# Third and fourth normalisation, step sizes and gate logits by batches in the experts' loop and the mixer's steps; batches stored singly

## The chip, the cores and the metric

The kernel runs on one core of a Trainium2 chip. The metric is the device time of one execution in microseconds (us). A core has five engines with a queue of instructions each: TensorE (PE: matrix products and transposes through the array into PSUM), VectorE (DVE), ScalarE (ACT), GpSimd (POOL) and SyncE (SP, which here issues the transfers by DMA). Each works through its own queue in order and waits for others by semaphores. SBUF is the working memory; PSUM holds eight banks of results.

## The reference, cut to what matters

```python
x = L0_attn_a_x                       # 8 x 512 x 128, float32
x = x + attention(layernorm(x))
x = x + experts(layernorm(x))
x = x + mixer(layernorm(x))
x = x + experts(layernorm(x))         # the same weights again

def layernorm(x):  return (x - mean(x)) / sqrt(var(x) + 1e-5)

def experts(x):                       # 4096 tokens, 8 experts
    probs = softmax(x @ wg)
    idx = argmax(probs)
    # a token is kept if it is among the first 512 of its expert
    gate = probs[idx] * kept
    return gate * (x @ W[idx].T + b[idx])

def mixer(u):                         # a state-space mixer, 8 heads
    z, xBC, dt = split(u @ W_in.T)
    dt = softplus(dt + dt_bias)
    x, B, C = split(silu(conv(xBC) + conv_b))
    y = scan(x * dt, A * dt, B, C) + x * Dskip
    return (layernorm(concat(y, z)) * ln_w + ln_b) @ W_out
```

## The kernel before

The stream x stays in SBUF for the whole program (`k.X`, named `stream` in the trace), 32 tiles of 128 tokens each, 128 wide. Four tiles are a group, which is also one of the 8 sequences. `k.XNT` (`stream_normed_t`) holds the normalised stream, turned, so that its tiles can go into TensorE. The stages come one after the other: attention, experts, mixer, experts. Within a stage each engine has its own program, written out by hand in the order in which the engine does it; there is no scheduler.

**Normalising.** The first two normalisations are done by groups inside other work, with the `group_` functions (L185 to L255): `group_stats` (DVE: four statistics L207, four merges L211, the variance L214), `group_rstd` (POOL, L220), `group_scale` (DVE, four operations L227), `group_turn` (PE, four transposes L238), `group_keep` (ACT, L245) and `group_products` (PE, L252: the matrix of 8 columns that the next stage needs, in bank 7). The third and fourth are done by `norm` (L1934) as stages of their own: `norm_vector`, `norm_gpsimd`, `norm_tensor` and `norm_scalar` (L99 to L177) take the stream in two halves. Behind them `eight_tensor` (L1222) multiplies all 32 tiles by a matrix of 8 columns: the mixer's raw step sizes behind the third, the gate logits of the second experts stage behind the fourth.

**Experts** (L1236). From the logits (L1315) a chain on DVE makes the gates (`gate8`, `experts_gate`; the last operation is L1340). Then a loop over the 8 groups, two at a time. SP copies the group's normalised tiles and its gates into small buffers (L1349, L1352). TensorE turns the gates (L1363), then for each tile makes two products of 512 columns, one for experts 0 to 3, "near", and one for 4 to 7, "far" (L1373), in two pairs of banks; behind the first tile come the products of gates and biases (L1382). DVE multiplies the near half by its gates out of PSUM (L1426), ScalarE the far half (L1401), and DVE adds the two (L1418); it also adds the biases to the stream (L1435). When the four tiles are there, POOL sums the eight experts' parts in two steps (L1448, L1451) and adds them to the stream (L1456).

A near bank is free for TensorE's next but one tile when DVE has multiplied (`near_scaled`), a far bank when ScalarE has (`far_scaled`).

**Mixer** (L1468). A chain on DVE makes the step sizes from the raw ones. Then steps, one for each sequence and shifted against each other: step i brings in sequence i+1 (projections, convolution), runs the scan over the tiles of sequence i, and finishes sequence i-1 (normalised y, output product, addition into the stream, L1877). At the end of a step DVE has in its queue the last addition L1877, the products behind the activations (L1817 to L1822) and the four operations of the normalised y (L1921).

**End.** `store_stream` (L1959) writes the whole stream by one transfer of 2048 KB.

## Time and profile before

| | us |
|---|---|
| median of 3 runs | 2992.06 (2991.2 to 2996.38) |
| profiled execution | 2988.63, of which its span 2986.9 |
| first experts stage: gates, loop | 2359.9 to 2369.5, to 2451 |
| third normalisation, step sizes' products | 2451 to 2473.4, to 2487.6 |
| mixer's steps | 2496.2 to 2850.6 |
| fourth normalisation, logits' products | 2850.9 to 2873, to 2887.3 |
| second experts stage: gates, loop | 2887.3 to 2896.9, to 2977.5 |
| store | 2977.8 to 2986.9 |

All before 2351 us is the attention and the first two normalisations. Over the whole span DVE is busy 90%, TensorE 85%, POOL 75% and ScalarE 69% of the time. These shares are those of the attention; the last fifth of the span is another program, and its stretches have to be read one by one. In the rows below a line such as "x4" puts several like instructions together: the time before the engine's name is then the sum of all of them. What stands in brackets at the end is how long the engine sat idle before, and what it waited for.

### The profile page before, as it was taken

The page shows a single profiled execution, that of the slowest core. Times are in us where ns is not written, and L with a number is a line of the kernel's source. Part 1 is how long each engine was busy: PE and PEld are TensorE (multiplying, and loading weights), DVE is VectorE, ACT ScalarE, POOL GpSimd, SP SyncE. Part 2 cuts the span into 40 slices and gives each one's busy share as a digit, 9 for nine tenths or more (in the row PEclk, how much of TensorE's full clock was granted, in tenths as well). Part 3 has the DMA queues.
Part 4 walks back from the last instruction along what each step waited for, and adds up shares of the span by engine and source line. Part 5 has one row for each costly group of instructions (what it writes and reads, how often), then busy time and mean ns, then how long its engine had stood idle before and what let it go on. Part 6 is the DMA issues. An engine that isn't in the chain of part 4 may idle for free. (4 is left out here: it accounts for less than half of the span.)

```text
span 2986.9 us, 56920 instructions
## 1 busy us (share of the span) xinstructions
PE 2534.7 (85%) x16480; PEld 1489.4 (50%) x16480; DVE 2680.1 (90%) x6614; ACT 2062.6 (69%) x6275; POOL 2254.1 (75%) x2816
## 2 busy tenths in 40 slices
PE   5788888888888888888888888888888777988857
PEld 3444444444444444444544444444444436777743
DVE  7999999999999999999999999999999374776546
ACT  3788888888888788888887878888887342222214
POOL 4899999998998999999999989999998251222105
PEclk8899999999999999999999999999999786776659
DMA  4444444444444444444444444444443000000001
GB/s 123 121 120 118 121 121 120 121 121 120 120 121 115 120 119 124 121 123 119 122 117 118 123 117 120 122 120 124 119 121 101 12 19 15 8 8 0 1 12 47
DMA packets 373454, 286.18 MB, mean 96 GB/s; under 512 B 30174, under 2 KB 369192, under 8 KB 373160
## 3 DMA queue, kind: packets, MB, share of 16 engines
q1 hardware_dynamic: 372232, 280.62, 33.0%
q8 instruction: 129, 2.11, 0.3%
q10 hardware_dynamic: 928, 2.10, 0.2%
q14 instruction: 165, 1.35, 0.1%
HBM read 139.48 MB, written 136.58 MB: 92 GB/s over the span
## 5 line engine op out<-in xcount | busy, mean ns | idle before, releaser
L1038 DVE MAX8 top<-work 128x8 f32<-128x512 f32 x1536 | 982.8, 684 | 0.0
L1047 DVE MATCH_REPLACE8 work<-top,work 128x512 f32<-128x512 f32 x1024 | 687.4, 682 | 0.0
L1124 POOL TENSOR_TENSOR scores<-scores,cut 128x512 f32<-128x512 f32 x512 | 642.0, 1276 | 0.0
L657 PE MATMUL bank<-probs_t,u 128*64 128x512 f32 x2048 | 476.8, 608 | 10.9 <-ACT u L893 1.4
L1116 POOL TENSOR_SCALAR cut<-scores,minus_max_and_least 128x512 f32<-128x512 f32 x512 | 354.2, 692 | 46.9
L945 ACT ACTIVATE probs_of_tile<-scores,minus_max_and_least 128x512 f32<-128x512 f32 x512 | 376.2, 767 | 14.4 <-POOL scores L1124 14.4
L1137 POOL TENSOR_SCALAR probs_of_tile<-probs_of_tile,inverse 128x512 f32<-128x512 f32 x512 | 349.2, 692 | 26.9 <-DVE inverse L1004 1.4
L1047 DVE MATCH_REPLACE8 work<-top,scores 128x512 f32<-128x512 f32 x512 | 343.6, 682 | 0.0
L1035 DVE MAX8 top<-scores 128x8 f32<-128x512 f32 x512 | 326.7, 683 | 5.2 <-ACT scores L886 4.9
L1120 POOL TENSOR_SCALAR cut<-cut 128x512 f32<-128x512 f32 x512 | 305.6, 613 | 21.5
L864 ACT ACTIVATE band<-band 128x129 f32<-128x129 f32 x512 | 155.2, 304 | 225.1 <-DMA band<-probs_scratch 224.2
L886 ACT ACTIVATE scores<-bank 128x512 f32<-128x512 f32 x512 | 273.3, 584 | 45.1 <-PE bank L706 45.0
L910 ACT ACTIVATE probs_t<-bank 128x512 f32<-128x512 f32 x512 | 282.0, 609 | 11.4 <-PE bank L753 10.3
L753 PE MATMUL bank<-identity,probs_of_tile 128*128 128x128 f32 x2048 | 278.4, 281 | 4.1 <-POOL probs_of_tile L1137 4.1
L657 PEld LDWEIGHTS bank<-probs_t,u 128*64 128x64 f32 x2048 | 137.8, 139 | 267.8 <-issue 228.0
L741 PE MATMUL bank<-identity,band 128*128 128x128 f32 x512 | 109.8, 297 | 185.5 <-ACT band L873 184.1
L657 PE MATMUL bank<-probs_t,v 128*64 128x384 f32 (+1 forms) x2048 | 255.4, 392 | 0.0
L753 PEld LDWEIGHTS bank<-identity,probs_of_tile 128*128 128x128 f32 x2048 | 242.7, 145 | 4.5 <-POOL probs_of_tile L1137 4.5
L657 PEld LDWEIGHTS bank<-probs_t,v 128*64 128x64 f32 x2048 | 124.3, 139 | 173.1 <-ACT probs_t L910 99.0
L1769 POOL TENSOR_TENSOR mixer_a_spread<-rest_after,mixer_a 128x1024 f32<-128x1024 f32 x32 | 66.4, 2075 | 168.8 <-PE bank L1626 137.6
L678 PE MATMUL bank<-keys_left,qt 64*128 64x64 f32 (+3 forms) x1024 | 185.5, 439 | 1.3 <-ACT scores L886 1.3
L923 ACT ACTIVATE rel<-bank 128x254 f32<-128x254 f32 x512 | 174.3, 414 | 1.9 <-PE bank L694 1.9
(274 smaller groups left out, 5005.6 us busy)
## 6 DMA issues: line engine op xcount, KB each, us to landing
probs_scratch<-probs_of_tile SPq DMA_DIRECT2D x256, 256.0 KB, 2.4
band<-probs_scratch SPq DMA_DIRECT2D x256, 256.0 KB, 3.2
rel_scratch<-rel SPq DMA_DIRECT2D x256, 254.0 KB, 3.1
relj<-rel_scratch SPq DMA_DIRECT2D x256, 128.0 KB, 2.3
relj<-rel_scratch SPq DMA_DIRECT2D x512, 64.0 KB, 2.4
experts_xs<-stream_normed_t SPq DMA_DIRECT2D x16, 256.0 KB, 2.3
stream<-in_L_attn_a_x SPq DMA_DIRECT2D x4, 512.0 KB, 7.9
mixer_xs<-stream_normed_t SPq DMA_DIRECT2D x8, 256.0 KB, 2.4
```

The costliest lines, as they stand in the source:

```text
L657: last = nc.tensor.matmul(U[HEADS[h], lo:hi], lhs, pt[mpar][:, h, jt, lo:hi], start=(jt == 0 and lo == 0), stop=(jt == NT - 1 and step > 0))
L753: last = nc.tensor.transpose(PT[h][:, jt * P:(jt + 1) * P], t.prob[Td][:, h, HALF + jt * P:HALF + (jt + 1) * P], k.ident[:, :])
L886: nc.scalar.activation(sc[Tb][:, h, :], SC[h][:, :], ACT.Copy).then_inc(s.scores_kept, 1)
L910: nc.scalar.activation(pt[dpar][:, h, :, Td * P:(Td + 1) * P], PT[h][:, :].rearrange("p (j i) -> p j i", j=NT), ACT.Copy).then_inc(s.probs ...
L945: nc.scalar.activation(t.prob[Tx][:, h, HALF:HALF + N], sc[Tx][:, h, :], ACT.Exp, bias=neg[q][:, h, 0:1], accum_out=rs[Tx][:, h:h + 1]).th ...
L1035: nc.vector.max(top[q][:, h, 0:8], sc[Tc][:, h, :]).then_inc(s.tops, 1)
L1038: nc.vector.max(top[q][:, h, 8 * rnd:8 * rnd + 8], work[:, h, :]).then_inc(s.next_tops, 1)
L1047: nc.vector.match_replace(out=work[:, h, :], in_to_replace=top[q][:, h, 8 * rnd:8 * rnd + 8], in_values=sc[Tc][:, h, :] if rnd == 0 else w ...
L1116: nc.gpsimd.tensor_scalar(cut[:, h, :], sc[Tc][:, h, :], neg[q][:, h, 1:2], STEEP, ALU.add, ALU.mult).then_inc(s.compared, 1)
L1120: nc.gpsimd.tensor_scalar(cut[:, h, :], cut[:, h, :], 0.0, NEG, ALU.min, ALU.max).then_inc(s.cut, 1)
L1124: nc.gpsimd.tensor_tensor(sc[Tc][:, h, :], sc[Tc][:, h, :], cut[:, h, :], ALU.add).then_inc(s.masked, 1)
L1137: nc.gpsimd.tensor_scalar(row, row, inv[Ty][:, h:h + 1], 1.0, ALU.mult, ALU.mult).then_inc(s.probs, 1)
```

## The change

`norm`, its functions, `eight_tensor`, `eight_vector` and `store_stream` are gone. The third normalisation is done by groups inside the first experts loop, the fourth inside the mixer's steps, with the `group_` functions; the raw step sizes and the gate logits come out of `group_products` or of its like in the mixer. All these loops are written out. In detail:

- *Experts' loop.* TensorE and ScalarE read `k.XNT` and `gate8` themselves; the small buffers and SP's copies are gone. The near half's product and the addition become one: four operations `scalar_tensor_tensor` of 128 columns, near out of PSUM times its gate plus the far half (L1299 of the changed kernel). The near bank is free after these (`summed`). The turned gates and the biases have one bank each instead of two, since one bank is needed for turning the group (TURN) and one for the 8-column products (EIGHT).
- *First experts loop only.* In group i DVE does the statistics of group i-1 behind the third tile and its scaling behind the fourth; POOL its `group_rstd` behind its addition; TensorE turns group i-2 between the gates' turns and the first tile and multiplies it behind the third tile; ScalarE keeps it behind the first tile. The last two groups are turned and multiplied behind the loop.
- *Mixer.* In step i DVE does the statistics of sequence i-1 behind the last addition into its stream and its scaling behind the normalised y. TensorE turns sequence i-2 before the projections, in their bank, and multiplies it at the step's end; ScalarE keeps the logits for the second experts stage. There is one step more.
- *Second experts loop.* SP stores each group, 256 KB, when its addition is done.

```diff
-            two_at_a_time(pe, GROUPS, body, with_half=True)
+            for i in range(GROUPS):
+                par = i % 2
+                if i:
+                    pe.wait_ge(g_kept, i)
                 for c in range(4):
-                    last = nc.tensor.transpose(ps[4 + par][0:E, c * P:(c + 1) * P], gs[par][:, c * E:(c + 1) * E],
-                                               k.ident[:, :])
+                    at = (i * 4 + c) * E
+                    last = nc.tensor.transpose(GT[0:E, c * P:(c + 1) * P], b.gate8[:, at:at + E], k.ident[:, :])
                 last.then_inc(g_turned, 1)
+                if follow and i >= 2:
+                    late(i - 2)
                 for c in range(4):
+                    t = i * 4 + c
                     for q in range(2):
-                            pe.wait_ge((near_scaled, far_scaled)[q], i * 4 + c - 1)
+                        if t >= 2:
+                            pe.wait_ge((summed, far_scaled)[q], t - 1)
...
+                    if c == 2 and follow and i >= 2:
+                        group_products(nc, pe, follow, i - 2, follow.W, k.XNT, EIGHT)
+            if follow:
+                for i in range(GROUPS - 2, GROUPS):
+                    late(i)
+                    group_products(nc, pe, follow, i, follow.W, k.XNT, EIGHT)
...
+            def scale(i):
+                if i >= 2:
+                    dve.wait_ge(follow.turned, i - 1)
+                group_scale(nc, dve, follow, gw, k.X, i, gw.xn[:, i % 2, :])
...
-                    nc.vector.tensor_tensor(near[c % 2][:, :].rearrange("p (e f) -> p e f", e=4),
-                                            ps[2 * (c % 2)][:, :].rearrange("p (e f) -> p e f", e=4),
-                                            b.gate8[:, bass.ds(t * E, 4)].unsqueeze(2).to_broadcast([P, 4, P]),
-                                            ALU.mult).then_inc(near_scaled, 1)
+                    for e in range(4):
+                        cols = slice(e * P, (e + 1) * P)
+                        last = nc.vector.scalar_tensor_tensor(
+                            out=sums[par][:, c, cols], in0=ps[2 * (c % 2)][:, cols],
+                            scalar=b.gate8[:, t * E + e:t * E + e + 1], in1=far[c % 2][:, cols],
+                            op0=ALU.mult, op1=ALU.add)
+                    last.then_inc(summed, 1)
...
+                    if c == 2 and follow and i:
+                        stats(i - 1)
+                if follow and i:
+                    scale(i - 1)
```

and in the mixer:

```diff
@@ TensorE
                     first_half(cur, par, 1)
+                if (done := i - 2) >= 0:
+                    if cur is not None:
+                        pe.wait_ge(m.conv_in, cur * 3 + 1)
+                    group_turn(nc, pe, follow, done, gw.xn[:, done % 2, :], PX, k.ident, 1)
                 if front is not None:
                     projections(front, 1 - par, pairs)
...
+                if done >= 0:
+                    pe.wait_ge(follow.kept, done + 1)
+                    if cur is not None:
+                        pe.wait_ge(m.turned_used, (cur + 1) * NT)
+                    for c in range(NT):
+                        t = done * NT + c
+                        last = nc.tensor.matmul(T1[:, 3 * P + c * E:3 * P + (c + 1) * E], k.XNT[:, t * P:(t + 1) * P],
+                                                follow.W, start=True, stop=True)
+                    last.then_inc(follow.products, 1)
@@ DVE
                     into_stream(NT - 1)
+                    dve.wait_ge(m.out_added, (back + 1) * NT)
+                    group_stats(nc, dve, follow, gw, k.X, back)
                 if front is not None:
                     silu(front, 1 - par)
...
+                if back is not None:
+                    if back >= 2:
+                        dve.wait_ge(follow.turned, back - 1)
+                    group_scale(nc, dve, follow, gw, k.X, back, gw.xn[:, back % 2, :])
```

What the change moves stands below at three places. In these lists a name behind `waits` is a semaphore, its first part the stage or normalisation that it belongs to. First TensorE at the start of a group of the first experts loop, before (the group's number is 1):

```order
L1363 MATMUL bank<-identity,experts_gs 8x128 [waits experts1_gs_in1]
L1363 MATMUL bank<-identity,experts_gs 8x128 x3
L1373 MATMUL bank<-rest_we,experts_xs 128x512 [waits experts1_near_scaled,experts1_xs_in1]
L1373 MATMUL bank<-rest_we,experts_xs 128x512 [waits experts1_far_scaled]
L1382 MATMUL bank<-rest_eb,experts_gt 128x128 [waits experts1_g_kept]
L1382 MATMUL bank<-rest_eb,experts_gt 128x128 x3
```

and on the same engine at the start of group 2 now:

```order
L1226 MATMUL bank<-identity,experts_gate 8x128 [waits experts1_g_kept]
L1226 MATMUL bank<-identity,experts_gate 8x128 x3
L132 MATMUL bank<-identity,group_xn 128x128 [waits norm3_scaled]
L132 MATMUL bank<-identity,group_xn 128x128 x3
L1235 MATMUL bank<-rest_we,stream_normed_t 128x512 [waits experts1_summed]
L1235 MATMUL bank<-rest_we,stream_normed_t 128x512 [waits experts1_far_scaled]
L1243 MATMUL bank<-rest_eb,experts_gt 128x128 [waits experts1_bias_added,experts1_g_kept]
L1243 MATMUL bank<-rest_eb,experts_gt 128x128 x3
```

The turn of the group before last (L132) now stands ahead of the first tile and waits for `norm3_scaled`; the first tile waits for `experts1_summed` instead of `experts1_near_scaled`.

Second, DVE at the end of group 1 of the same loop, before, where `bank0` and `bank2` are the near halves of the third and the fourth tile:

```order
L1426 TENSOR_TENSOR experts1_near0<-bank0,experts1_gate8 128x512 [waits experts1_summed,experts1_near_made]
L1418 TENSOR_TENSOR experts1_sums1<-experts1_near1,experts1_far1 128x512 [waits experts1_far_scaled,experts1_near_scaled]
L1426 TENSOR_TENSOR experts1_near1<-bank2,experts1_gate8 128x512 [waits experts1_summed,experts1_near_made]
L1418 TENSOR_TENSOR experts1_sums1<-experts1_near0,experts1_far0 128x512 [waits experts1_far_scaled,experts1_near_scaled]
L1418 TENSOR_TENSOR experts1_sums1<-experts1_near1,experts1_far1 128x512 [waits experts1_far_scaled,experts1_near_scaled]
```

and on DVE there now:

```order
L1299 SCALAR_TENSOR_TENSOR experts1_sums1<-bank0,experts1_gate8,experts1_far0 128x128 [waits experts1_far_scaled,experts1_near_made]
L1299 SCALAR_TENSOR_TENSOR experts1_sums1<-bank0,experts1_gate8,experts1_far0 128x128 x3
L101 BN_STATS group_stats<-stream 128x6 [waits experts1_stream_added]
L101 BN_STATS group_stats<-stream 128x6 x3
L105 BN_AGGR group_mean_var<-group_stats 128x2 [waits norm3_stats]
L105 BN_AGGR group_mean_var<-group_stats 128x2 x3
L108 TENSOR_SCALAR group_vareps<-group_mean_var 128x4 [waits norm3_merged]
L1299 SCALAR_TENSOR_TENSOR experts1_sums1<-bank2,experts1_gate8,experts1_far1 128x128 [waits experts1_far_scaled,experts1_near_made]
L1299 SCALAR_TENSOR_TENSOR experts1_sums1<-bank2,experts1_gate8,experts1_far1 128x128 x3
L121 TENSOR_SCALAR group_xn<-stream,group_mean_var,group_rstd 128x128 [waits norm3_rstd]
L121 TENSOR_SCALAR group_xn<-stream,group_mean_var,group_rstd 128x128 x3
```

The statistics of the group before stand between the third and the fourth tile, its scaling (L121) behind the fourth; every tile's first product waits for ScalarE's `far_scaled`.

Third, DVE at the end of a step of the mixer, before:

```order
L1877 TENSOR_TENSOR stream<-bank,stream 128x128 [waits mixer_out_made]
L1817 SCALAR_TENSOR_TENSOR mixer_x<-mixer_tanh_x,mixer_half_x 128x512 [waits mixer_squashed]
L1820 SCALAR_TENSOR_TENSOR mixer_b<-mixer_tanh_bc,mixer_half_bc 16x512 [waits mixer_squashed]
L1822 SCALAR_TENSOR_TENSOR mixer_c<-mixer_tanh_bc,mixer_half_bc 16x512
L1921 TENSOR_SCALAR mixer_yn<-mixer_yz,mixer_n_mean,mixer_n_rstd 128x256 [waits mixer_yn_turned,mixer_rstd]
L1921 TENSOR_SCALAR mixer_yn<-mixer_yz,mixer_n_mean,mixer_n_rstd 128x256 x3
```

and on DVE there now:

```order
L1773 TENSOR_TENSOR stream<-bank,stream 128x128 [waits mixer_out_made]
L101 BN_STATS group_stats<-stream 128x6 [waits mixer_out_added]
L101 BN_STATS group_stats<-stream 128x6 x3
L105 BN_AGGR group_mean_var<-group_stats 128x2 [waits norm4_stats]
L105 BN_AGGR group_mean_var<-group_stats 128x2 x3
L108 TENSOR_SCALAR group_vareps<-group_mean_var 128x4 [waits norm4_merged]
L1713 SCALAR_TENSOR_TENSOR mixer_x<-mixer_tanh_x,mixer_half_x 128x512 [waits mixer_squashed]
L1716 SCALAR_TENSOR_TENSOR mixer_b<-mixer_tanh_bc,mixer_half_bc 16x512 [waits mixer_squashed]
L1718 SCALAR_TENSOR_TENSOR mixer_c<-mixer_tanh_bc,mixer_half_bc 16x512
L1819 TENSOR_SCALAR mixer_yn<-mixer_yz,mixer_n_mean,mixer_n_rstd 128x256 [waits mixer_yn_turned,mixer_rstd]
L1819 TENSOR_SCALAR mixer_yn<-mixer_yz,mixer_n_mean,mixer_n_rstd 128x256 x3
L121 TENSOR_SCALAR group_xn<-stream,group_mean_var,group_rstd 128x128 [waits norm4_rstd,norm4_turned]
```

Nine operations of statistics stand ahead of the activations' products and four of scaling behind the normalised y.

## Rows read from the trace of the kernel before

**Rows 1.** Timeline at the third normalisation: start us, us, engine line operation.

```profile
2449.70 1.26 POOL L1456 TENSOR_TENSOR stream<-experts_one_sum,stream 128x512 f32 x1 [0.26 <-POOL experts_one_sum L1451]
...
2487.57 0.42 DVE L1233 COPY mixer_raw<-bank 128x256 f32<-128x256 f32 x1 [16.04 <-PE bank L1227]
```

**Rows 2.** Timeline at the fourth normalisation.

```profile
2850.25 0.29 DVE L1877 TENSOR_TENSOR stream<-bank,stream 128x128 f32<-128x128 f32 x1 [2.96 <-PE bank L1676]
...
2887.72 0.42 DVE L1317 TENSOR_REDUCE experts_top<-experts_logit 128x32 f32<-128x256 f32 x1
```

**Rows 3.** Timeline at the second normalisation's end, where the last group passes.

```profile
2349.28 0.60 PE L238 MATMUL bank<-identity,keys_left 128*128 128x128 f32 x4
...
2351.01 0.96 PE L252 MATMUL bank<-rest_wg,stream_normed_t 128*128 128x8 f32 x8
...
2351.46 0.87 DVE L207 BATCH_NORM_STATS2 group_stats<-stream 128x6 f32<-128x128 f32 x4 [20.36 <-POOL stream L1097]
...
2354.09 1.12 DVE L227 TENSOR_SCALAR keys_right<-stream,group_mean_var,group_rstd 128x128 f32<-128x128 f32 x4 [1.13 <-POOL group_rstd L220]
...
2355.26 1.11 PE L238 MATMUL bank<-identity,keys_right 128*128 128x128 f32 x4 [3.29 <-DVE keys_right L227]
...
2359.91 0.42 DVE L1315 COPY experts_logit<-bank 128x256 f32<-128x256 f32 x1 [4.70 <-PEq L582]
```

**Rows 4.** Timeline of one group in the first experts loop.

```profile
2418.11 1.88 PE L1373 MATMUL bank<-rest_we,experts_xs 128*128 128x512 f32 x4
...
2420.00 2.35 POOL L1448 TENSOR_TENSOR experts_two_sums<-experts_sums 128x1024 f32<-128x1024 f32 x1 [3.22 <-DVE experts_sums L1418]
...
2421.00 5.42 PE L1373 MATMUL bank<-rest_we,experts_xs 128*128 128x512 f32 x12
...
2423.23 1.14 ACT L1401 ACTIVATE experts_far<-bank,experts_gate 128x128 f32<-128x128 f32 x4 [1.88 <-PE bank L1373]
...
2428.58 2.35 POOL L1448 TENSOR_TENSOR experts_two_sums<-experts_sums 128x1024 f32<-128x1024 f32 x1 [3.22 <-DVE experts_sums L1418]
```

**Rows 5.** Busy time by stretch: the mixer's steps, one step's end.

```profile
core 0: us, PE busy (x) PEld busy (x) DVE busy (x) ACT busy (x) POOL busy (x), PEclk, DMA share, GB/s
2496.20:2850.60 354.40, 305.20 (x1568) 249.45 (x1568) 226.35 (x635) 94.40 (x184) 74.78 (x40) 0.69 0.02 7
2666.00:2676.00 10.00, 9.05 (x55) 6.58 (x54) 9.94 (x22) 3.96 (x7) 3.94 (x2) 0.94 0.00 0
```

**Rows 6.** Timeline at the first experts loop's start.

```profile
2369.10 0.42 DVE L1340 TENSOR_TENSOR experts_gate<-experts_keep,experts_prob 128x256 f32<-128x256 f32 x1
...
2370.03 0.55 SPq L1349 DMA_DIRECT2D experts_xs<-stream_normed_t  x1
...
2372.59 1.02 PE L1363 MATMUL bank<-identity,experts_gs 128*8 128x128 f32 x4 [7.51 <-DMA experts_gs<-experts_gate]
...
2373.40 3.62 PE L1373 MATMUL bank<-rest_we,experts_xs 128*128 128x512 f32 x4
```

**Rows 7.** Timeline in the mixer: DVE out of PSUM at 128 columns.

```profile
2633.84 0.28 DVE L1843 TENSOR_TENSOR mixer_dtx<-bank,mixer_dt 128x128 f32<-128x128 f32 x1
...
2634.04 0.28 DVE L1844 TENSOR_TENSOR mixer_yz<-bank,rest_dskip 128x128 f32<-128x128 f32 x1
```

**Rows 8.** Two lines at 38 us: durations in ns, least, median, most.

```profile
L227 DVE TENSOR_SCALAR probs_t<-stream,group_mean_var,group_rstd x4: 1291/1301/1307, 38.1 to 41.8; 128x128 f32<-128x128 f32 x4
L1068 POOL TENSOR_TENSOR stream<-stream,attention_out_bias x8: 1256/1262/1268, 38.1 to 46.6; 128x512 f32<-128x512 f32 x8
```

**Rows 9.** Timeline at one step's end in the mixer.

```profile
2667.08 3.02 DVE L1921 TENSOR_SCALAR mixer_yn<-mixer_yz,mixer_n_mean,mixer_n_rstd 128x256 f32<-128x256 f32 x4
...
2667.41 1.90 POOL L1769 TENSOR_TENSOR mixer_a_spread<-rest_after,mixer_a 128x1024 f32<-128x1024 f32 x1 [1.51 <-PE bank L1626]
```

**Rows 10.** Transfers: KB each, median us from issue to landing.

```profile
probs_scratch<-probs_of_tile SPq DMA_DIRECT2D x256, 256.0 KB, 2.4
out_stream<-stream SPq DMA_DIRECT2D x1, 2048.0 KB, 8.7
```

More of the change, by code:

```diff
@@ L1408, in _, with stats @@
+            if follow:
+                for i in range(GROUPS - 2, GROUPS):
+                    group_keep(nc, act, follow, i, TURN, k.XNT)
         @block.vector
         def _(dve):
-            def body(i, par, first):
-                def add(c):
-                    t = i * 4 + c
-                    dve.wait_ge(near_scaled, t + 1)
-                    dve.wait_ge(far_scaled, t + 1)
-                    if c == 0 and not first:
-                        dve.wait_ge(stream_added, i - 1)
-                    nc.vector.tensor_tensor(sums[par][:, c, :], near[c % 2][:, :], far[c % 2][:, :],
-                                            ALU.add).then_inc(summed, 1)
+            def stats(i):
+                dve.wait_ge(stream_added, i + 1)
+                group_stats(nc, dve, follow, gw, k.X, i)
@@ L1759, in body @@
                         keep_turned(back, c)
+                if done >= 0:
+                    act.wait_ge(follow.products, done + 1)
+                    nc.scalar.activation(follow.logits[:, done * NT * E:(done + 1) * NT * E],
+                                         T1[:, 3 * P:3 * P + NT * E], ACT.Copy).then_inc(m.logits_kept, 1)
             run_steps(act, body)
```

273 lines of the change are left out of this document (77 added, 196 removed).

## Prediction

> **What bounds the kernel now.** I read four views, in this order: busy time by stretch, the timeline at each seam, the timeline of one steady group of the experts' loop, and the costs of a few single forms. The attention, up to 2351 us, is not touched. The last 635 us are.
>
> At each of the two late normalisations the program stands. The third: the last addition into the stream ends at 2449.70 + 1.26 = 2450.96, and the raw step sizes are copied at 2487.57 [rows 1]. In these 36.6 us the whole stream is normalised, turned and multiplied. The fourth: 2850.25 + 0.29 = 2850.54 to the reduction of the logits at 2887.72, 37.2 us [rows 2]. What such a seam costs when the earlier groups have been done beforehand, the second normalisation shows, which already works so: from its last group's statistics at 2351.46 to the copy at 2359.91, 8.45 us [rows 3].
>
> In the experts' loop TensorE sets the pace. One group lies between POOL's two first sums at 2420.00 and 2428.58, 8.58 us; TensorE works in it from 2418.11 to 2426.42, 8.31 us, and the other engines have room [rows 4]. In the mixer no engine rules alone: TensorE is busy 305.20 of 354.40 us at a granted clock of 0.69, DVE 226.35, but in the ten microseconds at the end of a step DVE is busy 9.94 of 10.00 [rows 5].
>
> **The change part by part**, against the profiled execution (2988.63 us, which is 3.4 under the median of the runs).
>
> *Third normalisation's seam.* 36.6 us go, 8.45 come for the last group: **-28.2**. *Fourth:* 37.2 go; 8.45 come, with 0.2 for the hop to ScalarE, which now keeps the logits in the loop: **-28.5**.
>
> *The loads in front of the two loops.* The gates are done at 2369.10 + 0.42 = 2369.52, and TensorE starts at 2372.59, after the gates' transfer [rows 6]: 3.1 us. Now TensorE reads the gates directly. About 0.6 us stay for the start of the block; this estimate is the 0.5 us between the gates' end and the first transfer's issue at 2370.03 [rows 6], and a hop. **-2.5 twice, -5.**
>
> *The near half's bank, both loops.* It was freed by DVE's product alone. Now it is freed by four products of 128 columns which also add the far half, so they wait for ScalarE: 1.14 us for its four activations [rows 4]. Such a product of 128 columns with PSUM, a gate and an SBUF operand does not occur in the trace. Nearest are two forms from PSUM at 128 columns, 0.28 us each and 0.20 apart [rows 7]; the bounds are 4 x 0.20 and 4 x 0.34, and I take 1.1. With some 0.45 for three hops the bank is free 2.7 us after the far half is made; until then TensorE has one tile to do, 5.42 / 3 = 1.81 [rows 4]. Per group one tile pays the 0.9 in full (the third tile is covered by the bias products, the next group's first by the gates' turns). 8 x 0.9 = **+7** for the second loop, where this is all that happens; by the two bounds of the products it is +5 and +9.
>
> *The first loop's new wait.* This is the largest term. In group i TensorE, after turning the gates, has to turn the normalised group i-2 before its first tile. That group was scaled by DVE as its last work in group i-1, behind the products of the last tile. So TensorE can't run into group i while DVE finishes group i-1, as it does now; the engines go one after the other. The chain of one group is then:
> - TensorE from the first tile to the last: 8.31 as before [rows 4], and four products of the following stage, 0.96 [rows 3]: 9.3.
> - ScalarE 1.14, four products 1.1, hops 0.45: 2.7.
> - DVE's scaling, four operations on SBUF. Alone they take 1.12 [rows 3]. But here POOL starts its three sums at the same moment, because both are released by the same last product. Where the same scaling ran beside POOL's 1.26-us additions, at 38 us, each of the four took 1.30 instead of 0.28 [rows 8]: they went one and one. Here the first meets the sum of 2.35 us [rows 4], the other three the shorter ones: 2.35 + 3 x 1.29 = 6.2. Bounds 1.1 and 6.2. I take 6.2, as the row nearest in kind has no overlap left.
> - The turn, 0.60 at full clock [rows 3].
> - The clock. TensorE now sits idle 8.9 us (2.7 + 6.2) in each group. After an idle time of 7.51 us the first tile took 3.62 instead of 1.88 [rows 4, 6], and even after 3.29 us a turn took 1.11 instead of 0.60 [rows 3]: near the lower level (1.2 instead of 2.4 GHz). That is 1.7 + 0.5, **+2.2**.
>
> Sum 9.3 + 2.7 + 6.2 + 0.6 + 2.2 = 21.0 us a group, against 8.6: +12.4 for each of the groups 2 to 7, 74 us. The first two groups pay the bank's wait (+2) and the last group, whose chain begins after a late DVE, some +2 more (estimates): **+78**. The statistics (1.5 us: from 2351.46 to 2354.09 less the 1.13 that DVE then waits for POOL [rows 3]) stand behind the third tile and are covered: DVE waits there for TensorE. That two transfers a group fall away gives nothing more, since TensorE waited only for the first.
>
> *The mixer.* DVE gets, between the last addition of a step and the activations' products, statistics of 1.5 us, and behind the normalised y a scaling of 1.12 [rows 3]; both lie in the stretch where DVE is busy without a gap [rows 5], and the first matrices of the next step wait for the products behind it. 2.6 x 7 = 18. The four operations of the y, next to which it stands, take 3.02 beside POOL's spreading of 1.90 [rows 9], so the scaling may cost 3 instead of 1.1: upper bound 18 + 13. TensorE gets a turn and four products, 1.6 us a step; in the likeliest case they hide in the waits for DVE at a step's start, and at worst cost 11. Writing the loop out saves its branches, which show no time of their own. **+19.**
>
> *Storing singly.* One transfer of 2048 KB takes 8.7 us; one of 256 KB takes 2.4 [rows 10]. Seven of eight are issued a group apart, 9.5 us, and only the last is waited for: **-6**. The Trainium skill, "DMA: Bandwidth & Descriptors", section "Bandwidth", speaks against this: it tells one to batch transfers to 1 MiB or more. If the eight queued behind one another, at 2.4 each, they would end some 11 us later than the one. That would need a loop faster than its own transfers, and 9.5 is above 2.4.
>
> **Sum:** -28.2 - 28.5 - 5 + 7 + 78 + 19 - 6 = +36.3; 2988.6 + 36.3 = 3024.9, and with the 3.4 to the median 3028.
>
> **The rivals.** *Scaling and sums don't alternate.* If the four scalings come through in 1.1, a group costs 21.0 - 5.1 = 15.9, 7.3 more than now: 6 x 7.3 + 4 = 48 instead of 78, time 2998. For it: DVE has its scaling next in its own queue, while POOL needs a hop, so DVE may be through before POOL's first sum. Against it: the scaling at 38 us, where all four operations were stretched [rows 8].
> *The other side, faster.* Without the alternation TensorE's idle time is only 3.8 us a group. If the clock is held through that, the group costs 9.3 + 2.7 + 1.1 + 0.6 = 13.7, 5.1 more than now: 31 + 4 = 35. The sum is then -7 with the mixer at +19, and -21 if the mixer's added work fell into DVE's waits but for 5 us: 2971 to 2985. It decides where the group stays below 15 us: seams, loads and store give 67.7, the second loop and the mixer take 26, and of the 41.7 left 4 go to the loop's ends and 6.3 to each of six groups. Against it: the clock was down after 3.29 us of idling [rows 3].
> *The clock stays down through the whole first loop.* Then TensorE's 9.3 double, of which 1.7 are counted: (9.3 - 1.7) x 6 = 46, 3074. Against it: before, it came back one tile after the start.
> *The change doesn't do what it says:* if the waits for a former group left nothing early, the seams would stay at 37 and the added work come on top, over 3050. The order of the instructions speaks against it.
>
> **How the numbers follow.** Forecast as summed: 0.55, its own range 3005 to 3047 (the mixer from +5 to +36, the bank from +5 to +9, the scaling from 5 to 6.2). No alternation 0.17, split by its own width into slower 0.05, same 0.10, faster 0.02. Faster 0.18. Clock down 0.08. No effect 0.02. The predicted time is the forecast's, 3028. The range reaches down to 2978, into the middle of the faster case, and up to 3050: about 0.1 is left out on either side. A measurement of this kernel can tell some 0.2% from no change, 2986 to 2998. Faster 0.20, the same 0.10, slower 0.70.
>
> **What would show it.** In the changed kernel's first loop TensorE should wait, in front of the turn, for the scaled group, 8 to 9 us in each of six groups, and its first tile after that should be at half clock. The scaling should show four operations of over a microsecond while POOL sums. The second loop should have a period near 9.5. Both seams should be near 8.5. The steps of the mixer should grow by 2.6. The prediction is wrong if the scaling takes 1.1 and TensorE waits under 4 us, or if the turn finds its group already scaled.

## The result, and the profile after

The changed kernel takes 3027.43 us (median of 4 runs, 3012.61 to 3031.43) against 2991.63 us (median of 4, 2988.97 to 2996.38); the ratio is 1.0123, with a 95% interval from 1.0091 to 1.0156. It is slower, as forecast, and the time lies in the range. The ratio is taken over all runs of both kernels and can differ a little from the quotient of the medians, here and below. Its profiled execution has a span of 3022.6 us, 35.7 more than before. The stretches, each from one profile, ends taken from the last row of the stage:

| stretch | before | after | difference | forecast |
|---|---|---|---|---|
| attention up to the first gates' end | 2369.5 | 2359.3 | -10.2 | 0 |
| first experts loop (gates' end to last addition) | 81.4 | 163.4 | +82.0 | +75.5 |
| third normalisation's seam | 36.6 | 7.9 | -28.7 | -28.2 |
| step sizes and mixer | 363.0 | 385.8 | +22.9 | +19 |
| fourth normalisation's seam | 37.2 | 8.1 | -29.1 | -28.5 |
| second gates | 9.2 | 9.2 | 0 | 0 |
| second experts loop | 80.6 | 86.3 | +5.7 | +4.5 |
| store | 9.4 | 2.7 | -6.7 | -6 |

(The loops' forecasts contain the -2.5 of the loads.) The two seams answer [rows 1, 2]. The third, timeline:

```profile
2521.39 1.26 POOL L1332 TENSOR_TENSOR stream<-experts_one_sum,stream 128x512 f32<-128x512 f32 x1
...
2522.68 0.87 DVE L101 BATCH_NORM_STATS2 group_stats<-stream 128x6 f32<-128x128 f32 x4
...
2525.37 1.11 DVE L121 TENSOR_SCALAR group_xn<-stream,group_mean_var,group_rstd 128x128 f32<-128x128 f32 x4 [1.21 <-POOL group_rstd L114]
2526.55 1.11 PE L132 MATMUL bank<-identity,group_xn 128*128 128x128 f32 x4
...
2530.54 0.42 DVE L1382 COPY mixer_raw<-bank 128x256 f32<-128x256 f32 x1 [4.05 <-PEq L1205]
```

Only the last group's chain fills the seam, in the order of [rows 3]; the turn and the products of the group before it lie beside it. 2521.39 + 1.26 to 2530.54 is 7.9 us.

Where the time went, one group of the first loop shows, also timeline; it answers [rows 4]:

```profile
2426.15 0.60 PE L1226 MATMUL bank<-identity,experts_gate 128*8 128x128 f32 x4
...
2428.63 5.30 DVE L121 TENSOR_SCALAR group_xn<-stream,group_mean_var,group_rstd 128x128 f32<-128x128 f32 x4
2428.80 2.37 POOL L1324 TENSOR_TENSOR experts_two_sums<-experts_sums 128x1024 f32<-128x1024 f32 x1 [0.31 <-DVE experts_sums L1299]
2431.25 1.26 POOL L1327 TENSOR_TENSOR experts_one_sum<-experts_two_sums 128x512 f32<-128x512 f32 x1
2432.59 1.26 POOL L1332 TENSOR_TENSOR stream<-experts_one_sum,stream 128x512 f32<-128x512 f32 x1
2433.99 1.12 PE L132 MATMUL bank<-identity,group_xn 128*128 128x128 f32 x4 [7.24 <-DVE group_xn L121]
2434.90 3.62 PE L1235 MATMUL bank<-rest_we,stream_normed_t 128*128 128x512 f32 x4
...
2438.45 1.15 PE L1243 MATMUL bank<-rest_eb,experts_gt 8*128 8x128 f32 x8
...
2439.53 3.70 PE L1235 MATMUL bank<-rest_we,stream_normed_t 128*128 128x512 f32 x8
...
2448.44 2.37 POOL L1324 TENSOR_TENSOR experts_two_sums<-experts_sums 128x1024 f32<-128x1024 f32 x1 [0.31 <-DVE experts_sums L1299]
```

TensorE has turned the gates at 2426.75 and stands until the scaling is done, 7.24 us. The four scaling operations last 5.30 us, to 2433.93; POOL's third sum ends at 2433.85. Then the turn takes 1.12 and the first tile 3.62, near half speed, and the group comes to 2448.44 - 2428.80 = 19.6 us. The next one takes 23.3. Busy time by stretch for these two (columns as in [rows 5]):

```profile
2428.80:2448.44 19.64, 12.41 (x40) 6.40 (x40) 11.64 (x31) 5.49 (x18) 5.91 (x4) 0.83 0.00 0
2448.44:2471.70 23.26, 16.02 (x40) 8.22 (x40) 11.65 (x31) 5.49 (x18) 5.92 (x5) 0.63 0.00 0
```

TensorE, DVE and ScalarE do the same work in both (POOL's fifth instruction in the second is cut by the stretch's edge); the granted clock is 0.83 and 0.63. The waits of TensorE over the whole loop and the seam behind it, by cause (us in total, times, longest):

```profile
PE bank L132 <- DVE group_xn L121: 51.6, 7, 7.7
PE bank L1235 <- DVE experts_sums L1299: 1.5, 2, 0.7
```

### The profile page after: what moved, and what is told of

Read it like the earlier page. It is cut to its first block and busy times, and to the rows that moved or that the text cites. A ratio compares the mean times of both kernels' runs of the same rounds, so it can differ in the third digit from the quotient of the medians.

```text
span 3022.6 us, 55798 instructions
## 1 busy us (share of the span) xinstructions
PE 2553.1 (84%) x16480; PEld 1492.0 (49%) x16480; DVE 2686.3 (89%) x6791; ACT 2062.5 (68%) x6283; POOL 2259.2 (75%) x2828
## 5 line engine op out<-in xcount | busy, mean ns | idle before, releaser
L932 DVE MAX8 top<-work 128x8 f32<-128x512 f32 x1536 | 1065.6, 792 | 0.0
L941 DVE MATCH_REPLACE8 work<-top,work 128x512 f32<-128x512 f32 x1024 | 742.5, 790 | 0.0
L839 ACT ACTIVATE probs_of_tile<-scores,minus_max_and_least 128x512 f32<-128x512 f32 x512 | 376.4, 767 | 17.5 <-POOL scores L1018 17.5
L941 DVE MATCH_REPLACE8 work<-top,scores 128x512 f32<-128x512 f32 x512 | 370.9, 788 | 0.0
L929 DVE MAX8 top<-scores 128x8 f32<-128x512 f32 x512 | 353.7, 789 | 0.1
L647 PE MATMUL bank<-identity,probs_of_tile 128*128 128x128 f32 x2048 | 272.1, 277 | 4.0 <-POOL probs_of_tile L1031 4.0
L941 DVE MATCH_VALUE_LOAD work<-top,work 128x8 f32 x1024 | 195.2, 191 | 0.0
```

The costliest lines, as they stand in the source:

```text
L647: last = nc.tensor.transpose(PT[h][:, jt * P:(jt + 1) * P], t.prob[Td][:, h, HALF + jt * P:HALF + (jt + 1) * P], k.ident[:, :])
L839: nc.scalar.activation(t.prob[Tx][:, h, HALF:HALF + N], sc[Tx][:, h, :], ACT.Exp, bias=neg[q][:, h, 0:1], accum_out=rs[Tx][:, h:h + 1]).th ...
L929: nc.vector.max(top[q][:, h, 0:8], sc[Tc][:, h, :]).then_inc(s.tops, 1)
L932: nc.vector.max(top[q][:, h, 8 * rnd:8 * rnd + 8], work[:, h, :]).then_inc(s.next_tops, 1)
L941: nc.vector.match_replace(out=work[:, h, :], in_to_replace=top[q][:, h, 8 * rnd:8 * rnd + 8], in_values=sc[Tc][:, h, :] if rnd == 0 else w ...
```

## The experiments

Theory A is the prediction's: the third normalisation makes the engines hand on to each other in the first loop. TensorE waits in front of its first tile for the scaling, the scaling is stretched by POOL's sums, and TensorE's clock is down afterwards. Rivals: B, the added work itself fills the group; C, the clock alone makes it long. The kernel before was run beside them on each chip and lay at 2973.8 to 2986.3 there (medians of 8 to 16 runs), so kernels from different chips are compared by their ratio to it.

| run | median us | range | before on that chip | ratio (95% interval) |
|---|---|---|---|---|
| e1, sums behind scaling | 2978.6 | 2976.2 to 2987.0 | 2986.3 | 0.9967 (0.9952 to 0.9982) |
| e2, turn behind second tile | 2973.1 | 2972.0 to 2977.0 | 2986.3 | 0.9958 (0.9944 to 0.9973) |
| e3, third apart | 2983.3 | 2975.8 to 2986.8 | 2986.3 | 0.9983 (0.9972 to 0.9995) |
| e4, scaling beside statistics | 2951.9 | 2946.6 to 2957.1 | 2986.3 | 0.9887 (0.9868 to 0.9906) |
| e5, TensorE busy | 2990.8 | 2985.2 to 2991.8 | 2973.8 | 1.0052 (1.0027 to 1.0078) |
| e8, buffers kept | 3023.0 | 3010.0 to 3028.7 | 2973.8 | 1.0152 (1.0113 to 1.0190) |
| e9, changed kernel again | 3018.3 | 3010.3 to 3024.3 | 2973.8 | 1.0149 (1.0116 to 1.0183) |
| e6, more statistics | 2967.7 | 2952.0 to 2976.5 | 2981.6 | 0.9955 (0.9932 to 0.9978) |
| e7, near apart | 2938.2 | 2933.2 to 2940.5 | 2981.6 | 0.9856 (0.9834 to 0.9878) |
| e10, before again | 2979.9 | 2975.6 to 2986.0 | 2979.4 | 1.0001 (0.9983 to 1.0020) |
| e11, fourth apart | 2944.7 | 2932.3 to 2950.4 | 2979.4 | 0.9877 (0.9838 to 0.9915) |
| e12, near apart again | 2942.3 | 2932.4 to 2945.8 | 2979.4 | 0.9880 (0.9851 to 0.9908) |

**e1: the sums behind the scaling.**

```diff
                 if i:
                     pool.wait_ge(stream_added, i)
+                    if follow:
+                        pool.wait_ge(follow.scaled, i)
                 nc.gpsimd.tensor_tensor(two_sums[:, :, :, :], four[:, :, 0:2, :], four[:, :, 2:4, :],
```

> The changed kernel with one wait more: in the first experts loop POOL starts a group's sums only when DVE's scaling of the group before is done. Theory A (TensorE waits in front of its first tile for the scaling, and the scaling is stretched because it alternates with POOL's sums): the four scaling operations fall from 5.3 to 1.1 us, TensorE's wait in front of the turn from 7.2 to some 3.0, each of seven groups is 4.2 us shorter, with up to 1.7 more where a tile gets its full clock back: 29 to 39 us off, 2988 to 2998. Rival B (the new work of DVE and the later release of the banks fill the group by themselves, and the alternation lies beside them): no change within 5 us, 3022 to 3032; or slower by the 1.1 us a group that the sums start later.

One wait more makes the kernel some 47 us faster than the changed one (0.9967 against 1.0123 of before). Theory B falls, since the added work is all still there. A is right in kind, and its forecast of 29 to 39 us was too small. The first of the two groups below, timeline, takes 13.3 us:

```profile
2432.96 0.66 PE L132 MATMUL bank<-identity,group_xn 128*128 128x128 f32 x4 [3.05 <-DVE group_xn L121]
2433.08 2.35 POOL L1326 TENSOR_TENSOR experts_two_sums<-experts_sums 128x1024 f32<-128x1024 f32 x1 [1.43 <-DVE group_xn L121]
2433.45 1.88 PE L1235 MATMUL bank<-rest_we,stream_normed_t 128*128 128x512 f32 x4
...
2445.11 1.10 DVE L121 TENSOR_SCALAR group_xn<-stream,group_mean_var,group_rstd 128x128 f32<-128x128 f32 x4
2446.27 1.11 PE L132 MATMUL bank<-identity,group_xn 128*128 128x128 f32 x4 [3.05 <-DVE group_xn L121]
2446.38 2.34 POOL L1326 TENSOR_TENSOR experts_two_sums<-experts_sums 128x1024 f32<-128x1024 f32 x1 [1.43 <-DVE group_xn L121]
```

The scaling takes 1.10 and the wait 3.05, as expected. What I had not counted is the clock: after the same idle time of 3.05 us the turn took 0.66 in one group and 1.11 in the next. The seven groups took 11.3, 14.9, 15.1, 13.0, 13.3, 17.8 and 13.3.

**e2: the turn behind the second tile.**

```diff
-                if follow and i >= 2:
-                    late(i - 2)
...
+                    if c == 1 and follow and i >= 2:
+                        late(i - 2)
-                    if c == 2 and follow and i >= 2:
+                    if c == 3 and follow and i >= 2:
                         group_products(nc, pe, follow, i - 2, follow.W, k.XNT, EIGHT)
```

> The changed kernel with TensorE's turn of group i-2 moved from in front of group i's first tile to behind its second, the 8-column products from behind the third tile to behind the fourth, ScalarE's copy with them. The scaling stays where it is, stretched by POOL. Theory A: TensorE makes two tiles while DVE scales; what is left of a group is DVE's chain, 5.3 of scaling, 1.1 and 0.7 for the first tile and the biases, 3.3 until the third tile is there, 1.1, 1.4 of statistics, 1.1, some 13 to 14 us instead of 22.4: six groups give 50 to 56, 2971 to 2977. Rival B (the work fills the group): the group stays over 20 us, 3015 or more. Rival C (the clock is what makes the groups long, not the wait): the group falls by no more than 4, 3003 or more.

As theory A has it, and against C: groups of 13.1, 13.4, 15.3, 14.9, 14.6 and 13.4 us, 2973.1. The scaling is as long as ever; it only isn't waited for:

```profile
2429.06 5.39 DVE L121 TENSOR_SCALAR group_xn<-stream,group_mean_var,group_rstd 128x128 f32<-128x128 f32 x4
2429.08 2.34 POOL L1324 TENSOR_TENSOR experts_two_sums<-experts_sums 128x1024 f32<-128x1024 f32 x1
...
2430.57 1.98 PE L1233 MATMUL bank<-rest_we,stream_normed_t 128*128 128x512 f32 x4
...
2434.50 0.66 PE L132 MATMUL bank<-identity,group_xn 128*128 128x128 f32 x4 [1.95 <-DVE group_xn L121]
```

TensorE makes tiles while DVE scales, and 1.95 us of the wait are left.

**e3: the third normalisation put back as a stage of its own.**

```diff
-            norm3.W = r.wdt[:, :]
-            experts(nc, sem, allocate(ctx), ps, k, r, "experts1", norm2, norm3, gw)
+            experts(nc, sem, allocate(ctx), ps, k, r, "experts1", norm2)
+        norm(nc, norms, ps, k, w)
```

> The changed kernel with the third normalisation and the step sizes' products put back as stages of their own, by the code of before; the fourth, the stores and the near halves stay changed. If the first loop's loss is the handing on of the third normalisation and nothing else, this loop takes what the second one does, 86 us instead of 163, and the seam is 36.6 again instead of 7.9: 77 off, 29 on, 2979. If the loss came from the near halves' product or from reading gates and stream directly, the loop stays well over 100 us, and the time at 3000 or more.

All seven groups of the first loop take 9.6, the loop 86.8, the seam 36.4; the time, 2983.3, is 4 above the expected. So of the first loop's 82 us the third normalisation makes 76.6 (163.4 against 86.8); the rest is the near bank's, as in the second loop.

**e4: both ends moved.**

```diff
                     if c == 2 and follow and i:
+                        dve.wait_ge(stream_added, i)
+                        if i >= 2:
+                            scale(i - 2)
                         stats(i - 1)
-                if follow and i:
-                    scale(i - 1)
```

and on TensorE and ScalarE the turn of group i-3 behind the second tile, its products behind the fourth.

> The changed kernel with both ends moved in the first loop: DVE scales group i-2 in group i right before the statistics of i-1, when POOL has no sum to make, and TensorE turns group i-3 behind the second tile of group i. Theory A: scaling 1.1, no wait in front of the first tile, a group of 9.6 to 10.5 like the second loop's: 70 to 75 off and 2 to 4 on for a third group after the loop, 2955 to 2962, faster than the kernel before. Rival B: DVE has 7.7 us of work in a group, which stand between tiles, so that the tiles are released later: 12 or more a group, 2975 or more. Rival C: the clock does not come back, 18 or more a group, 3000 or more.

Groups of 10.1 to 10.4, the loop 94.9, and 2951.9: faster than the kernel before by 1.1% (0.9 to 1.3). The time is 3 us below the expected range, but on this chip the kernel before is some 5 us faster too. The scaling is short and nobody waits for the turn:

```profile
2419.73 0.60 PE L132 MATMUL bank<-identity,group_xn 128*128 128x128 f32 x4
...
2424.38 1.10 DVE L121 TENSOR_SCALAR group_xn<-stream,group_mean_var,group_rstd 128x128 f32<-128x128 f32 x4
```

**e5: TensorE kept busy.** Seven products whose results are overwritten, in front of the turn:

```diff
                 if follow and i >= 2:
+                    if i >= 3:
+                        pe.wait_ge(follow.kept, i - 2)
+                    for n in range(7):
+                        nc.tensor.matmul(TURN[:, :], k.XNT[:, i * 512:i * 512 + P], r.we[:, 0:512], start=True, stop=True)
                     late(i - 2)
```

> The changed kernel with seven products of 512 columns more in front of each of the six turns that wait, written into the turn's bank, which the turn then overwrites: TensorE works through most of the 7.2 us in which it waited, and nothing else is moved. Theory: of the changed kernel's 22.4 us a group some 4 to 5 are the lower clock after the wait (the groups took 19.6 to 23.7, and those with one slow tile less were the shorter). With TensorE working the turn takes 0.6 and the first tiles 1.9, a group 17 to 18: 25 to 32 off the changed kernel, 2995 to 3002. Rival: the clock has nothing to do with it and the length is all waiting: no change within 5 us of the changed kernel in this call, or longer where the added products end after the scaling.

The kernel does more and is faster by 27 us than the changed kernel on the same chip (2990.8 against 3018.3). All six groups take 17.5:

```profile
2404.77 0.66 PE L132 MATMUL bank<-identity,group_xn 128*128 128x128 f32 x4 [1.24 <-DVE group_xn L121]
2405.27 1.88 PE L1239 MATMUL bank<-rest_we,stream_normed_t 128*128 128x512 f32 x4
...
2414.86 6.17 PE L1232 MATMUL bank<-rest_we,stream_normed_t 128*128 128x512 f32 x14
...
2416.91 5.30 DVE L121 TENSOR_SCALAR group_xn<-stream,group_mean_var,group_rstd 128x128 f32<-128x128 f32 x4
```

The added products are those of L1232; the scaling is stretched as before, and the turn waits for it. But the turn takes 0.66 and the first tile 1.88. So of a group's 21 to 22 us some 4 to 5 are the clock, and 17.5 are what the work and the handing on take at full clock, against 9.6 without the third normalisation (e3). C holds for the smaller part.

**e6: more statistics in the mixer**, on e4's kernel.

```diff
                     dve.wait_ge(m.out_added, (back + 1) * NT)
+                    for n in range(8):
+                        t = back * NT + n % NT
+                        nc.vector.bn_stats(spare[:, n, :], k.X[:, t * D:(t + 1) * D])
                     group_stats(nc, dve, follow, gw, k.X, back)
```

> The kernel of the fourth experiment with eight statistics more, into a spare buffer, in front of the eight group statistics of the mixer's steps: 8 x 0.21 us, 1.7 us of DVE more a step at the very place where the change put its 1.5. Theory D (the end of a step is DVE's, as the prediction had it): every step grows by 1.7, 12 to 14 us in all, 2964 to 2966. Rival E (once the steps run at some 44.5 us, TensorE at its lower clock sets their length and DVE's work lies beside it; only the steps before that and the last grow): 2 to 7 us, 2954 to 2959, and the steps of 44.5 stay as they are.

Neither theory holds as a whole. The time is some 20 us above e4's by the ratios (0.9955 against 0.9887), more than D would have it, but runs of this kernel lie 24 us apart. In its profile the fourth to the seventh step stay at 44.4, as E would have it, and the first three grow to 41.4, 44.0 and 47.3 (e4: 39.0, 40.3, 44.1). So the steps of 44.4 have room for 1.7 us more of DVE at this place. What makes the others longer stays open.

**e7: the near half's product and addition apart in the second loop**, on e4's kernel.

```diff
-                            pe.wait_ge((summed, far_scaled)[q], t - 1)
+                            pe.wait_ge((near_scaled if out is not None else summed, far_scaled)[q], t - 1)
```

and DVE's instructions for this loop as they were before.

> The kernel of the fourth experiment with the near halves' product and their addition apart again in the second experts loop, as in the kernel before, so that a near bank is free after DVE's product alone. If the later release of the near bank is what makes a group 9.60 instead of 8.58, the loop falls to 8.6 a group: 7 to 8 off, 2944 to 2945. If the direct reading of gates and stream or the single banks for gates and biases make it, a group stays at 9.6: no change within 2.

All seven groups of the second loop take 8.6 and the loop 77.8 instead of e4's 87.7. Two of POOL's first sums, timeline, in the changed kernel's second loop:

```profile
2957.31 2.35 POOL L1324 TENSOR_TENSOR experts_two_sums<-experts_sums 128x1024 f32<-128x1024 f32 x1 [4.56 <-DVE experts_sums L1299]
...
2966.91 2.35 POOL L1324 TENSOR_TENSOR experts_two_sums<-experts_sums 128x1024 f32<-128x1024 f32 x1 [4.57 <-DVE experts_sums L1299]
```

and in e7's:

```profile
2886.93 2.35 POOL L1354 TENSOR_TENSOR experts_two_sums<-experts_sums 128x1024 f32<-128x1024 f32 x1 [3.21 <-DVE experts_sums L1289]
...
2895.51 2.35 POOL L1354 TENSOR_TENSOR experts_two_sums<-experts_sums 128x1024 f32<-128x1024 f32 x1 [3.21 <-DVE experts_sums L1289]
```

The loop's added microsecond a group is the near bank's later release. At 2938.2 this is the lowest median of all kernels here, 1.4% (1.2 to 1.7) under the kernel before, though its interval overlaps that of e4; run again as e12, 1.2% (0.9 to 1.5):

> The kernel of the seventh experiment, unaltered, beside the two others on one chip: 2933 to 2941 as then, groups of 10.1 to 10.4 us in the first experts loop and 8.6 in the second, steps between 375 and 386, gates done between 2358 and 2363.

In e12's profile the gates were done at 2356.3, below the expected 2358; its median is 1 us above the expected range, and the loops' groups are as expected.

**e8, e9 and e10: the 10 us of the attention.** e8 allocates the former buffers again, without using them; e9 and e10 are the changed kernel and the one before, unaltered.

> The changed kernel with the buffers of the former normalisation still allocated at their old place and not used, so that what is allocated behind them has its old addresses. In the two profiles the first experts stage's gates were done 10.2 us earlier in the changed kernel, at 2359.3 instead of 2369.5, though all before that is the same code. Theory (addresses): gates done at 2367 to 2370 here, the time 8 to 10 above the changed kernel in this call. Rival (one execution differs from another by that much): gates at any time between 2358 and 2370, the time within 5 of the changed kernel.

> The changed kernel itself, unaltered, for comparison on the same chip: by its first measurement 3012 to 3031, its median 3027. By the theory on addresses its gates are done within 2 us of 2359.3; by the rival they may be done up to 10 later.

> The kernel before, unaltered, for a second profile of it. In nine profiles of kernels with the changed mixer its steps take 375 to 386 us, 381 in the mean, against 363.0 in the one profile of before. If the added work makes that difference, the steps take 360 to 367 here again; if one execution differs from another by that much, they may take up to 380. By the theory on addresses the first experts stage's gates are done between 2365 and 2370, as in the three profiles of kernels that hold the old buffers, and not between 2358 and 2363 as in the seven that do not.

The gates were done at 2365.8 in e8 and 2359.7 in e9, which spoke for the addresses. But e10, with the very code of before, had them done at 2361.2, against 2369.5 in its first profile: the same program differs by 8 us there from one execution to another, and the times of e8 and e9 agree within their intervals. So the 10.2 us are not shown to be the addresses'. Nor is an effect of theirs excluded: on each of the three chips that ran both kinds, every kernel that holds the old buffers had its gates done later than every one that doesn't, by 5 to 9 us. That is 2368.0 (e3) against 2358.9 to 2362.9 (e1, e2, e4), 2365.8 (e8) against 2358.4 and 2359.7 (e5, e9), and 2361.2 and 2363.2 (e10, e11) against 2356.3 (e12). With one profile each this stays open.

**e11: the fourth normalisation put back as a stage of its own**, on e7's kernel.

```diff
-            mixer(nc, sem, allocate(ctx), ps, k, r, norm3, norm4, gw)
+            mixer(nc, sem, allocate(ctx), ps, k, r, norm3, None, gw)
+        norm(nc, norms, ps, k, w)
```

> The kernel of the seventh experiment with the fourth normalisation and the gate logits put back as stages of their own, by the code of before, so that the mixer's steps are those of before. Theory (the mixer pays 18 for the fourth normalisation and the seam gives 29): steps 363 instead of 381, the seam 37.2 instead of 8.1: 5 to 17 slower than the seventh experiment's kernel in this call, some 2949. Rival (the steps' length comes from the clock and not from the added work, they take 375 to 386 without it too): the whole seam is lost, 25 to 30 slower, 2965.

2944.7 against e12's 2942.3: no difference that these runs can tell. In the profiles the seam is 36.8 against 8.1, and step sizes and mixer take 353.1 against 376.7. So what the seam gives, 29 us, the mixer takes back all but some 5. The theory's 5 to 17 us in the whole time don't show. The rival falls: without the added work the stretch is short, 363.0, 360.9 (e10) and 353.1, while the ten profiles with the fourth normalisation in it and nothing added (the changed kernel, e1 to e5, e7, e8, e9, e12) lie between 375.2 and 385.8, 380.7 in the mean. The steps of e11 do the work of those of before, but they are written out like the changed kernel's, where the kernel before has a loop for the middle ones. So e11 against e12 shows the added work by itself, 23.6 us. Whether the 8 to 10 us by which e11 lies under the kernel before come from the writing out, one profile doesn't show.

## Why the prediction was right, point by point

**The seams, the loads, the store**: -28.7, -29.1, 0.5 us in place of 3.1 in front of each loop, and -6.7. All as worked out. The loads at the first loop, timeline; it answers [rows 6]:

```profile
2358.86 0.43 DVE L1201 TENSOR_TENSOR experts_gate<-experts_keep,experts_prob 128x256 f32<-128x256 f32 x1
...
2359.83 1.01 PE L1226 MATMUL bank<-identity,experts_gate 128*8 128x128 f32 x4 [5.00 <-PEq L1152]
```

The last 256 KB are through 2.7 us after the last addition, where the one large transfer was through 9.4 after it. Of the eight small ones seven lie beside the loop, and they don't queue up: they land 2.3 us after their issue in the median, and are issued 9.6 apart.

**The near bank.** A group of the second loop takes 9.60 instead of 8.58, 1.0 each where I had 0.9; the four products take 1.13 together (forecast 1.1). e7 shows the cause.

**The first loop's wait.** This is the step that decided the sign, and it went as described: the turn in front of the first tile, waiting for a scaling that is last in DVE's row, stretched by POOL (e1, e2, e3). Of its terms the scaling was 5.30 and not 6.2: it starts 0.17 us ahead of POOL's first sum, so the first of the four passes freely, and the last ends with POOL's last sum. The wait was 7.24 and not 8.9; the forecast had not taken off the gates' turns (0.60), which TensorE does before it. The clock was mis-sized the other way: I had one turn and one tile at the lower level, 2.2 us. In the changed kernel sometimes the biases' products and the second tile were slow too. This is the row of the group that begins at 2406.76, timeline:

```profile
2412.86 3.62 PE L1235 MATMUL bank<-rest_we,stream_normed_t 128*128 128x512 f32 x4
2416.42 2.07 PE L1243 MATMUL bank<-rest_eb,experts_gt 8*128 8x128 f32 x8
...
2418.42 5.17 PE L1235 MATMUL bank<-rest_we,stream_normed_t 128*128 128x512 f32 x8
```

The biases take 2.07 instead of the 1.15 at 2438.45, and the next two tiles 5.17 instead of the 3.70 at 2439.53. By e5 the clock's share is 4 to 5 us a group. The two errors, -0.9 and +2 to 3, partly cancelled, which is luck: 21.0 forecast, 22.4 measured in the mean of groups 2 to 7, and 21.2 in e9's profile. How many products are slow differs from execution to execution: the loop took 163.4, 157.2 and 159.9 us in the changed kernel's two profiles and in e8's. The 19 us by which runs of the changed kernel spread are not explained by that, since the kernel before spreads by 16 to 25 us on the other chips too.

**The mixer.** The total was near, +22.9 in the first profile, and +18.7 between the mean of the ten profiles and that of the two of the kernel before (363.0 and 360.9). The working was not, so the agreement is luck: "2.6 x 7" lets every step grow alike. Busy time by stretch, for the second step, the seventh, and the last to its last addition, columns as in [rows 5]. Before:

```profile
2551.18:2590.93 39.75, 37.37 (x202) 29.93 (x202) 27.22 (x80) 11.78 (x23) 8.66 (x5) 0.70 0.02 7
2756.93:2801.28 44.35, 38.88 (x196) 32.27 (x196) 28.61 (x81) 11.79 (x23) 9.51 (x5) 0.69 0.00 0
2801.28:2850.54 49.26, 37.13 (x173) 29.94 (x172) 20.00 (x73) 9.71 (x22) 2.90 (x2) 0.59 0.00 1
```

After:

```profile
2596.53:2642.94 46.41, 42.83 (x198) 34.44 (x198) 29.84 (x94) 11.78 (x23) 11.39 (x6) 0.61 0.02 7
2816.70:2861.19 44.49, 39.71 (x208) 33.25 (x208) 30.91 (x94) 12.58 (x25) 10.16 (x6) 0.69 0.00 1
2861.19:2916.37 55.18, 42.68 (x192) 35.39 (x192) 22.44 (x86) 10.99 (x25) 4.16 (x3) 0.57 0.00 1
```

The seventh step holds more operations of DVE (94 against 81, busy 30.91 against 28.61) and is as long as before, 44.5 against 44.4. The second grew by 6.7, with the clock at 0.61 instead of 0.70, and the last, to the last addition, by 5.9. DVE's time at a step's end is not simply added: in e6 the steps of 44.4 took 1.7 us more of it without growing. The steps fall between some 39 and some 46 us, and TensorE's clock goes with that only in part: 39.75 us at 0.70 and 46.41 at 0.61, but 44.35 at 0.69. What sets in which length a step falls I did not find out: e6 was to show it and didn't. The forecast put the writing out of the loop at nothing; by e11 it may have saved some 8 to 10 us, and the added work then cost 24 (e11 against e12). e11's later steps are at 39.3 to 42.1, where the kernel before and all kernels with the changed mixer come to 44.4 or 44.5.

**What was not forecast.** The attention was 10.2 us shorter in the first profile of the changed kernel. The unaltered kernel differs there by 8 us between two profiles (e10), and what the buffers' addresses add is open. The 10.2 us came close to hiding +6.5 in the first loop and +3.9 in the mixer: the profile's sum of 35.7 agrees with the forecast's 36.3 better than its terms do. Without the attention that profile is 45.9 us longer, and on e9's chip the changed kernel's median is 44.5 us above that of before (3018.3 against 2973.8). So the meeting of 3028 and 3027 is in part luck; the sign and the mechanism of the largest term are not.

**The rivals.** "Scaling and sums don't alternate" did not happen: the scaling starts only 0.17 us before POOL's first sum, so only its first operation gets through (0.34 us). The faster case's group, 13.7 us, was worked out for a scaling of 1.1 and a held clock: e1 made just that, and its groups with a held clock take 13.0 to 13.3. The faster side was thus one wait away.

## What to carry to other kernels

Work that is slipped into a loop must be asked not only how long it is, but behind what it stands on the engine that does it, and in front of what on the engine that needs it: the same instructions cost 82 us here with the taker at the head of the next group, and 9 to 14 with both ends moved (the loops of e4, e7 and e12, 90.7 to 94.9 against 81.4). Where the slipped-in work reads SBUF on DVE, put it where POOL is idle. And a seam that is filled is not a seam won: in the profiles of e11 and e12 the fourth normalisation gave 29 us at the seam and cost 24 in the mixer, and whether it pays could not be told from the whole time.

## What the runs showed of the hardware

- A wait of 3.05 us left TensorE's turn at 0.66 in one group and 1.11 in the next (e1), so one row of a slow turn after such a wait, as in [rows 3], doesn't say that the clock always falls. Seven products that nobody needs, in a wait of 7.24 us, shortened the program by 27 us (e5).
- Four scaling operations that take 1.10 us together with POOL idle (e1) took 5.30 beside three sums of POOL and ended with the last of them, though they began first. The shortest of the four took 0.34 us and the longest 2.37, as long as POOL's first sum. The Trainium skill, "SBUF — State Buffer", section "Who interferes with whom", says that such a DVE instruction can need the ports it shares with GpSimd, and that whoever issues first holds them for the whole instruction while the other blocks. The rows agree that DVE's instruction waits out a whole sum, and show that the two take turns instruction by instruction, so that here DVE's row of short instructions ended with POOL's long ones.
- The same program had the first experts stage's gates done at 2369.5 and at 2361.2 in two profiles (before and e10), so here terms below some 10 us can't be read from two profiles' absolute times, but only from the lengths of the stretches that the change touches.
